# A recurrent kernel's update gate: high and low part of the state share one pass over the high weights

## The reference

```python
z = sigmoid([x_t, h] @ Wz);  r = sigmoid([x_t, h] @ Wr)
c = tanh([x_t, r * h] @ Wh)
h_new = (1 - z) * h + z * c
h_next = tanh(h_new @ Wp) if t % 4 == 3 and t < 127 else h_new
out[:, t] = x[:, t] + h_new
```

## Time and profile before

| | us |
|---|---|
| median of 3 runs (lowest, highest) | 1050.49 (1050.46, 1051.28) |
| profiled execution | 1050.32 |
| its span | 1048.5 |
| PE busy in the span | 1043.2 (99%) |
| DVE busy | 760.1 (72%) |
| ACT busy | 730.9 (70%) |
| mean granted TensorE clock | 0.999 |

### The profile page before, as it was taken

The page is one execution under the profiler, slowest core; times in us unless marked ns, Lnnn a source line. Parts: engine busy times, 40 slices in busy tenths (PEclk is TensorE's granted clock), DMA queues, the critical chain, the costliest instruction groups (busy, mean ns, idle before and its releaser), DMA issues.

```text
span 1048.5 us, 54202 instructions
## 1 busy us (share of the span) xinstructions
PE 1043.2 (99%) x24039; PEld 966.7 (92%) x24039; DVE 760.1 (72%) x2611; ACT 730.9 (70%) x1789; POOL 0.2 (0%) x4
## 2 busy tenths in 40 slices
PE   9999999999999999999999999999999999999998
PEld 4577999999999999999999999999999999999998
DVE  6978888777777676776777767777777776666665
ACT  6777777766776777667676777767776677665665
POOL 0000000000000000000000000000000000000000
PEclk9999999999999999999999999999999999999999
DMA  9212211101111001111001110011110100000001
GB/s 329 109 62 64 83 53 44 43 10 37 43 43 44 23 23 44 43 43 43 22 25 44 43 43 24 23 44 43 43 43 15 31 23 24 23 23 23 23 4 44
DMA packets 38507, 47.65 MB, mean 45 GB/s; under 512 B 2177, under 2 KB 34049, under 8 KB 37889
## 3 DMA queue, kind: packets, MB, share of 16 engines
q1 hardware_dynamic: 38272, 44.19, 12.5%
HBM read 27.40 MB, written 16.78 MB: 42 GB/s over the span
## 4 chain that ended last, share of the span: by engine, by line
PE 99%; ACT 1%; DVE 0%; issue 0%; ACTq 0%
PE acc L1255 55%; PE x_acc L1170 34%; PE x_acc L1067 8%; PE x_acc L1190 1%; ACT wrec_hi L595 0%; PE acc L1183 0%; PE acc L1073 0%; PE x_acc L1177 0%; ACT gate L548 0%; ACT acc L574 0%; ACT x_part L481 0%; ACT gate L595 0%; DVE new L1006 0%; ACT gate L684 0%; DVE x_blk L1009 0%
## 5 line engine op out<-in xcount | busy, mean ns | idle before, releaser
L548 ACT ACTIVATE gate<-acc,unscale 128x128 f32<-128x128 f32 x700 | 237.3, 383 | 236.0 <-PE acc L1255 235.6
L1255 PE MATMUL acc<-h_split,wrec_hi 128*128 128x64 f16 x8192 | 343.4, 193 | 0.0
L1170 PE MATMUL x_acc<-x_hi,win_hi 128*128 128x256 f16 x1092 | 297.7, 273 | 0.0
L1170 PE MATMUL x_acc<-x_hi,win_lo 128*128 128x256 f16 x1092 | 297.6, 273 | 0.0
L1170 PE MATMUL x_acc<-x_lo,win_hi 128*128 128x256 f16 x1092 | 297.6, 273 | 0.0
L1255 PEld LDWEIGHTS acc<-h_split,wrec_hi 128*128 128x128 f16 x8192 | 282.9, 98 | 0.0
L1255 PE MATMUL acc<-q_split,wrec_hi 128*128 128x64 f16 x5088 | 215.3, 193 | 0.0
L1255 PE MATMUL acc<-h_split,wrec_lo 128*128 128x64 f16 x4096 | 203.2, 193 | 0.0
L514 ACT ACTIVATE x_part<-x_acc,bias,part_unscale 128x256 f32<-128x256 f32 x312 | 158.9, 560 | 45.2 <-PE x_acc L1170 45.2
L1255 PEld LDWEIGHTS acc<-q_split,wrec_hi 128*128 128x128 f16 x5088 | 179.0, 98 | 0.0
L574 ACT ACTIVATE acc<-x_part,seed_scale 128x256 f32<-128x256 f32 x383 | 172.8, 478 | 2.1 <-ACT x_part L514 0.4
(11 more groups left out here) (135 smaller groups left out, 1080.2 us busy)
## 6 DMA issues: line engine op xcount, KB each, us to landing
out_dram<-x_blk SPq DMA_DIRECT2D x30, 512.0 KB, 3.2
x_blk<-x_dram SPq DMA_DIRECT2D x24, 512.0 KB, 4.1
x_blk<-x_dram SPq DMA_DIRECT2D x3, 1024.0 KB, 9.1
x_part<-wz_dram SPq DMA_DIRECT2D x4, 256.0 KB, 6.8
x_part<-wh_dram SPq DMA_DIRECT2D x4, 256.0 KB, 6.8
x_part<-wr_dram SPq DMA_DIRECT2D x1, 1024.0 KB, 11.3
x_part<-wz_dram SPq DMA_DIRECT2D x1, 1024.0 KB, 13.5
x_part<-wh_dram SPq DMA_DIRECT2D x1, 1024.0 KB, 15.7
```

Source lines behind the costliest of these rows:

```text
L548: nc.scalar.activation(gate[g][:, half, :], acc[g][:, half, :], func, scale=unscale[:, g:g + 1]).then_inc(gate_ready[g], 1)
L1170: mm = nc.tensor.matmul(in_halves(x_acc[bank][:])[:, j], weights[g][:, slot_w, k, j * P:(j + 1) * P], in_halves(values[m % 2][:, slot_x, : ...
L1255: mm = nc.tensor.matmul(bank[:, j, :], weights[g][:, k, j * P:(j + 1) * P], values[:, k, lo, :], start=False, stop=False, skip_group_check ...
```

## The change

A new constant `JOINT_FROM = 16` and `joint(t)`, true for 16 <= t < 126. In these 110 steps:

- PE: the two passes of Z over the high weights become one: the moving operand is `h_split[:, k]`, high and low part side by side (128 columns), and the result goes to both halves of Z's bank. All of Z's matmuls stand before C; none is left behind.
- DVE: after the low part of r*h it waits for `product_done[Z]` and adds the two halves into `gate[Z]` with a `tensor_reduce`. `split_slot` moves from before the Z gate to after the output of the step (L1031), ahead of scales, sums and `end_quarter`.
- ACT: the sigmoid of Z waits for that sum and works in place in `gate[Z]`. Z's seed writes both halves, 512 columns, each scaled with half the factor.

```diff
+JOINT_FROM = 16
+        half_seed_scale = sb("half_seed_scale", [P, 1])
+        def joint(t):
+            return JOINT_FROM <= t < T - 2
 # ACT
+            def squash_sum(t):
+                act.wait_ge(update_summed, t - JOINT_FROM + 1)
+                nc.scalar.activation(gate[Z][:], gate[Z][:], ACT.Sigmoid, scale=unscale[:, Z:Z + 1]).then_inc(gate_ready[Z], 1)
 # in seed(g, t)
+                if g == Z and joint(t):
+                    act.wait_ge(half_seed_scale_ready, 1)
+                    nc.scalar.activation(acc_bank[Z][:], added.unsqueeze(1).broadcast_to([P, 2, KC, B]), ACT.Copy,
+                                         scale=half_seed_scale[:, 0:1]).then_inc(seed_ready[Z], 1)
+                    return
-                squash(Z, ACT.Sigmoid, t, WHOLE)
+                if joint(t):
+                    squash_sum(t)
+                else:
+                    squash(Z, ACT.Sigmoid, t, WHOLE)
 # DVE
-                for block_m, slot in slots_at(t):
-                    split_slot(block_m, slot)
+                if joint(t):
+                    dve.wait_ge(product_done[Z], t + 1)
+                    nc.vector.tensor_reduce(flat(gate[Z][:]), acc_bank[Z][:].rearrange("p n k b -> p (k b) n"), AX_X, ALU.add).then_inc(update_summed, 1)
+                else:
+                    for block_m, slot in slots_at(t):
+                        split_slot(block_m, slot)
+                if t == JOINT_FROM - 2:
+                    nc.vector.tensor_scalar(half_seed_scale[:], seed_scale[:, Z:Z + 1], 0.5, None, ALU.mult).then_inc(half_seed_scale_ready, 1)
 # DVE, after the output of the step (L1031)
+                if joint(t):
+                    for block_m, slot in slots_at(t):
+                        split_slot(block_m, slot)
 # PE
+            def update_both(k_of):
+                for k in k_of:
+                    for j in range(KC):
+                        mm = nc.tensor.matmul(acc_bank[Z][:, :, j, :], wrec_hi[Z][:, k, j * P:(j + 1) * P], h_split[:, k],
+                                              start=False, stop=False, skip_group_check=True)
+                return mm
-                behind = t < T - 2
+                behind = t < T - 2 and not joint(t)
+                if joint(t):
+                    rec(Z, wrec_lo, h_split, HIGH, 0)
+                    update_both(range(KC)).then_inc(product_done[Z], 1)
+                else:
 # (the passes as before)
```

More of the change, by code:

```diff
@@ L347, in gru_kernel @@
         q_hi_ready, q_full_ready, q_lo_ready = sem("q_hi_ready"), sem("q_full_ready"), sem("q_lo_ready")
+        half_seed_scale_ready, update_summed = sem("half_seed_scale_ready"), sem("update_summed")
         keep_ready, new_ready = sem("keep_ready"), sem("new_ready")
@@ L1284, in _ @@
                 rec(R, wrec_hi, h_split, HIGH, 1).then_inc(product_done[R], 1)
[L1286 to L1290, removed]
-                behind = t < T - 2
-                if not behind:
-                    rec(Z, wrec_hi, h_split, HIGH[1:], 1).then_inc(product_done[Z], 1)
+                behind = t < T - 2 and not joint(t)
[3 more added lines that the diff above has]
+                else:
+                    rec(Z, wrec_hi, h_split, LOW, 0)
+                    rec(Z, wrec_lo, h_split, HIGH, 0)
+                    rec(Z, wrec_hi, h_split, HIGH, 0)
+                    rec(Z, wrec_hi, h_split, LOW, 1)
+                    rec(Z, wrec_hi, h_split, HIGH[:1], 1)
+                    if not behind:
+                        rec(Z, wrec_hi, h_split, HIGH[1:], 1).then_inc(product_done[Z], 1)
                 if t == 1:
```

## The result

| | before | changed |
|---|---|---|
| median, us (lowest to highest, 11 runs each) | 1050.74 (1049.93 to 1052.01) | 1053.35 (1052.68 to 1053.79) |
| profiled execution / its span | 1050.32 / 1048.5 | 1053.46 / 1051.6 |
| busy in the span: PE, DVE, ACT | 1043.2, 760.1, 730.9 | 1041.6, 820.5, 741.3 |

The change makes the kernel slower by 2.6 us, a ratio of 1.0023 (95% interval 1.0015 to 1.0031). The forecast was 1053.6 us, 0.25 us above the measured median.

What follows compares the result with a forecast made beforehand. PE, busy 1043.2 of 1048.5 us, bounds the kernel: -4.1 us of PE work, +6.4 us at product 7 and +0.8 us in the last two blocks make +3.1 us, 1053.6 us. Own range 1051.5 to 1056.5 us, over the cases 1047.0 to 1058.5 us.

Steps and rivals of the forecast that it cites:

- PE's saving: Z's high-weight passes on PE: one wide matmul saves 2.4 ns over two narrow ones, 4.1 us in all.
- The rivals in which it saves nothing: Z's wide matmul on PE takes as long as two narrow ones: 1057.7 us, chance 0.06.
- in which weight loads show: On PE, weight loads show behind wide matmuls, 16 x 40 ns a step, 70 us: 1120 us, chance 0.01.
- C's place: On PE, C begins 0.08 us later behind R and ends 0.04 us earlier in the step.
- The sum and the gate: On DVE the reduce takes 0.69 us; Z's sigmoid on ACT and what follows it come 0.31 us late.
- the rival of a slow reduce: DVE's reduce is slow because its pairs lie 256 elements apart: 1069.4 us at half rate, chance 0.10.
- Product 7: Last step of a block: PE waits 0.58 us for DVE's end_quarter, in eleven steps, 6.4 us.
- The rival in which this wait stays covered: PE's product 7 never waits for end_quarter; only PE's saving and the tail remain: 1047.2 us, chance 0.15.
- The other steps of the blocks: Outside a block's last step, the split's 0.66 us and the 0.31 us shift fall into DVE's idle time: no cost.
- waits in other steps of the blocks 2 to 13: Sign that the forecast is wrong: waits show in those blocks in steps other than the ones it named.
- The last blocks: Steps 112 to 125: waits before the state of 0.24, 0.19 and 0.12 us, ACT 0.2 us in step 125; 0.8 us.
- the tail: Waits of the last two blocks, steps 112 to 125, step 125's ACT cost included: 0.8 us.

Runs made afterwards that it cites:

- narrow experiment: The changed kernel with two matmuls of 64 columns for each wide one, into the same two halves: 1057.56 us, ratio 1.0063 to the kernel before.
- the first and the fourth experiment: First: changed kernel, slot split behind end_quarter in a block's last step, 1047.45 us. Fourth: kernel before, only the slot split moved behind the output, 1053.09 us.
- half-sum experiment: The changed kernel with the sum of Z's two halves replaced by a copy of the first half, gate values wrong: 1048.66 us, ratio 0.9982.
- the first two experiments: Changed kernel, first with the slot split behind end_quarter in a block's last step, 1047.45 us; second with every slot split back ahead of the sum, 1053.83 us.

## Why the prediction was right, step by step

**PE's saving** was put at 4.1 us; it is 4.2 us by the distances, and the narrow experiment shows the same distances side by side. The matmul that writes two pieces costs what the one-piece rows said. The rivals in which it saves nothing, or in which weight loads show, are out.

**C's place.** C begins 2.76 us after R in every step from 16 to 109, against 2.68 us before, and ends 0.04 us earlier: as worked out.

**The sum and the gate.** The reduce takes 0.68 us (0.69 forecast) over 110 times, from PSUM, with 256 pairs that lie 256 elements apart; the rival of a slow reduce is out. It starts behind the low part of r*h, with 0.01 us of gap. Counted from R's first matmul, `keep` is 0.32 us later than before (0.31 forecast). Two small errors nearly cancel: ACT starts 0.03 us after DVE's end (0.04 forecast) and the sum is 0.01 us shorter, while the sigmoid from SBUF takes 507 ns where the one from PSUM took 473 ns.

**Product 7.** The step that was to decide did. 0.53 us each against 0.58 us: 0.04 us of the difference is the time to go on, 0.06 us at all of them, where I had taken the middle between 0.06 and 0.15 us. Eleven of them, none in step 111. The rival in which this wait stays covered is out; the first and the fourth experiment show from both sides what its cover holds and that the queue ahead of `end_quarter` is what empties it.

**The other steps of the blocks** were put at nothing, and in the steps 16 to 108 nothing it was, with one step forgotten:

**Step 110 is the miss.** I costed ACT at nothing up to step 124, by its total idle time and by step 63, and listed no step in which its idle time is short. The period of eight that I read into the steps 16 to 111 doesn't hold here: in step 109 ACT has two x splits of block 15 after the seeds. The prediction had named waits in other steps of the blocks 2 to 13 as a sign that it is wrong. Step 110 lies in block 13, so by that sign it was wrong here, if only by 0.46 us. ACT in the kernel before, from step 109's seeds, then ACT and PE in the changed kernel up to step 110's candidate:

```profile
921.40 0.87 ACT L574 ACTIVATE acc<-x_part,seed_scale 128x256 f32<-128x256 f32 x2
922.20 1.33 ACT L466 ACTIVATE x_hi<-x_blk,x_scale 128x512 f16<-128x512 f32 x2
```

```profile
924.19 0.69 ACT L582 ACTIVATE acc<-x_part,half_seed_scale 128x512 f32<-128x512 f32 x1
924.80 1.33 ACT L473 ACTIVATE x_hi<-x_blk,x_scale 128x512 f16<-128x512 f32 x2
...
926.54 1.01 ACT L521 ACTIVATE x_part<-x_acc,bias,part_unscale 128x256 f32<-128x256 f32 x2
927.44 0.47 ACT L591 ACTIVATE acc<-x_part,seed_scale 128x256 f32<-128x256 f32 x1
927.84 0.62 ACT L560 ACTIVATE gate<-acc,unscale 128x128 f32<-128x128 f32 x2
```

```profile
927.29 1.06 PE L1292 MATMUL acc<-h_split,wrec_hi 128*128 128x128 f16 x16
928.67 0.39 PE L1284 MATMUL acc<-q_split,wrec_lo 128*128 128x64 f16 x8 [0.32 <-DVE q_split L997]
```

In both kernels splits, reads, seed and gate of R follow without a gap, so whatever ACT is late after the Z gate reaches PE: 0.49 us from start to start, where the kernel before already waited 0.09 us. The two traces give the parts. Counted from the first matmul of step 109, ACT begins the seeds 0.23 us later than before, because of the late gate. The instruction behind the wide seed starts 0.61 us after it; behind a narrow one it is 0.40 us. That is 0.44 us in all. PE asks for its operand 0.04 us later than before: R begins 0.04 us sooner, C 0.08 us later behind it. 0.09 + 0.44 - 0.04 = 0.49 us. The half-sum experiment shortens the sum alone, and its 0.27 us go out of this wait.

**The last blocks.** In step 123 0.23 us (0.19 forecast), in step 112 0.16 us (0.12), 0.05 us in each of five more, 0.28 us in step 125 (0.2). The wait of 0.16 us for r*h that the kernel before has in step 112 is gone in the changed one. Step 115 was put at 0.24 us and measures 0.45 us. DVE:

```profile
964.86 0.48 DVE L986 TENSOR_TENSOR q_split<-q_full,q_split 128x128 f16<-128x128 f32 x2
965.44 0.69 DVE L1010 TENSOR_REDUCE gate<-acc 128x256 f32<-128x512 f32 x1
```

The reduce starts 0.58 us after the pair ahead of it, in step 63 0.41 us. These 0.17 us are most of the 0.21 us over the forecast; the rest is the time to go on, 0.15 us where I had taken 0.10 us. Of the 110 steps only step 77 has the same 0.17 us, and there it stays covered. PE's wait in step 115 is 0.44 to 0.45 us in the first two experiments too, so it belongs to the program and not to one execution. No semaphore explains the pause. But the trace's record of transfers has a clue: a load on one of the two queues of kind `instruction` (q14) starts 0.7 us after the end of each of these two pauses. From step 16 on, DVE pauses ten times in this way between instructions that otherwise follow one another closely, for 0.17 to 0.35 us, and each time such a load starts 0.6 to 1.0 us later; the pause in step 55 of the experiment with only the split moved has one 0.7 us later. That DVE passes there from one loaded stretch of its program to the next would fit. No run tests it, so the cause stays open.

Together the tail, step 110 included, is 1.7 us where 0.8 us was forecast, and product 7 is 5.8 us where 6.4 us was: the errors of +0.9 and -0.6 us nearly cancel, by luck, and make the forecast look better than its steps.

## What to carry to other kernels

Where PE is busy 99% of the time, list for every wait its cover in ns, not only that it is zero: here eleven places had 0.40 us while the first use of the new state had 1.2 us and more in every step from 16 to 108, and a change that put 0.98 us into a queue paid, in those steps, only at the eleven. A late engine is to be followed through its queue up to the next semaphore that PE waits for, and the item to move is whatever stands ahead of that and isn't needed first; turning round two instructions in one step of eight turned the loss of 2.6 us into a gain of 3.4 us. Merging two matmuls with one stationary tile saves only a fixed part, 2.4 ns each here, so it pays only if everything that it drags along stays under cover.

## What the runs showed of the hardware that was not expected

A matmul of 128 columns that writes two pieces of 64 columns, 1 KB apart in a bank, has the same distance as one that writes a single piece: 55.9 ns (1760 of them) against 55.9 ns. A `tensor_reduce` over pairs, 512 elements from PSUM to 256, takes 682 ns, less than a 512-element reduce to one from SBUF (689 ns); a copy of 256 elements from PSUM takes 416 ns. The sigmoid of 256 elements in place in SBUF takes 507 ns, the same from PSUM 473 ns. PE's first matmul after a wait for DVE came 0.06 us after DVE's recorded end at product 7 and at the low part of r*h (steps 65 and 110), but 0.15 us after it at the first high part that R, C or PROP needs (steps 110, 112 and 115, among others); no run tells why. DVE pauses for 0.17 to 0.35 us at ten places of the changed kernel behind step 16 with no wait to explain it; what the trace has beside them is told under the last blocks.
